# Four message-passing layers on a graph: the edge-MLP pass fetches three of every 32 chunks of source rows by products with node masks, and ScalarE's two relus change places

## The reference, cut to what matters

```
xi = x[dst]
xj = x[src]
h = jnp.concatenate([xi, xj - xi], axis=-1)
h = jax.nn.relu(h @ W1 + b1)
h = jax.nn.relu(h @ W2 + b2)
out = jax.ops.segment_max(h, dst, num_segments=x.shape[0])
```

## Time and profile before

| | |
|---|---|
| median of three runs | 10778.5 us |
| the profiled execution's own time | 10698.97 us |
| its span, first to last instruction | 10697.2 us |
| busy: PE / DVE / ACT / POOL | 4797.8 / 4232.9 / 1862.9 / 6552.4 us |
| granted TensorE clock, mean over the span | 0.653 |

### The profile page before, as it was taken

One profiled execution on the slowest core, in us unless ns is written; L12 is line 12 of the kernel. 1 busy time (PEld: TensorE's weight loads), 2 busy tenths in 40 slices (PEclk: granted clock), 3 DMA queues, 4 the chain that ended last, 5 costly groups with the idle time before them and its releaser, 6 DMA issues.

```text
span 10697.2 us, 122041 instructions
## 1 busy us (share of the span) xinstructions
PE 4797.8 (45%) x31058; PEld 3606.8 (34%) x31058; DVE 4232.9 (40%) x8620; ACT 1862.9 (17%) x5090; POOL 6552.4 (61%) x6391
## 2 busy tenths in 40 slices
PE   3788455555555457777777411211112311211111
PEld 3677444444444435555555211111111111111110
DVE  7899544445444554444444211212212111211212
ACT  0677223223322200000000100000000100000000
POOL 8333466666666545666665466666666566666666
PEclk9999655555555578898889655555555655555555
DMA  6000133333333312222222222222222222222222
GB/s 262 23 15 15 38 87 89 89 88 90 89 89 88 80 45 64 64 64 65 64 64 65 81 58 56 60 55 59 59 54 59 87 56 59 58 57 57 58 58 55
DMA packets 491880, 728.06 MB, mean 68 GB/s; under 512 B 143188, under 2 KB 206036, under 8 KB 488933
## 3 DMA queue, kind: packets, MB, share of 16 engines
q0 software_dynamic: 204288, 216.96, 11.8%
q1 hardware_dynamic: 159948, 245.16, 7.3%
q10 hardware_dynamic: 127584, 265.22, 6.5%
HBM read 421.77 MB, written 305.03 MB: 68 GB/s over the span
## 4 chain that ended last, share of the span: by engine, by line
another core or an unknown queue 36%; issue 21%; PE 21%; DVE 11%; POOL 4%; ACT 3%; DVEq 2%; DMA 2%; ACTq 0%; SPq 0%; POOLq 0%
PE ps L1672 8%; PE ps L1736 3%; DVE scn L1328 2%; PE ps L1704 2%; PE ps L1581 2%; PE ps L1548 1%; DVE shared L1308 1%; POOL big L723 1%; PE ps L1553 1%; DVE idx L1293 1%; POOL big L786 1%; DMA flags<-keep_and_type_rows 1%; DVE picked_nodes L1267 1%; POOL gat L776 1%
## 5 line engine op out<-in xcount | busy, mean ns | idle before, releaser
L776 POOL DMA_INDIRECT gat<-typed_table,idx x3128 | 2997.6, 958 | 1569.8 <-issue 918.2
L776 POOL DMA_INDIRECT gat<-node_table,idx x2835 | 2732.4, 964 | 1753.7 <-issue 857.7
L1736 PE MATMUL ps<-ident,scn 128*128 128x128 f32 x3136 | 938.3, 395 | 3543.4 <-DVE scn L1328 2335.8
L1328 DVE TENSOR_TENSOR_SCAN scn<-flags,scn,ps 128x256 f32<-128x256 bf16 x1176 | 874.0, 743 | 3510.1 <-remote 2966.3
L1736 PEld LDWEIGHTS ps<-ident,scn 128*128 128x128 f32 x3136 | 566.8, 226 | 3843.3 <-issue 3825.9
L863 ACT COPY dmp<-ps 128x256 f32<-128x256 f32 x1568 | 586.6, 374 | 6316.6 <-remote 3885.0
L1672 PE MATMUL ps<-big 128*128 128x320 bf16 x8820 | 1454.7, 319 | 147.1 <-issue 73.4
L1672 PEld LDWEIGHTS ps<-big 128*128 128x128 bf16 x8820 | 915.5, 104 | 550.3 <-issue 179.3
L1704 PE MATMUL ps<-ident,gat 128*128 128x128 f32 x3136 | 888.3, 380 | 443.2 <-DVE gat L1298 299.0
L1721 PE MATMUL ps<-shared,bd_w 128*128 128x256 f32 x784 | 447.6, 673 | 988.8 <-issue 596.2
L1704 PEld LDWEIGHTS ps<-ident,gat 128*128 128x128 f32 x3136 | 529.6, 193 | 558.9 <-issue 507.1
(11 more groups left out here) (287 smaller groups left out, 6087.5 us busy)
## 6 DMA issues: line engine op xcount, KB each, us to landing
scan_rows<-dmp ACTq DMA_DIRECT2D x784, 256.0 KB
flags<-keep_and_type_rows SPq DMA_DIRECT2D x980, 128.0 KB
spread_table<-tsl ACTq DMA_DIRECT2D x101, 576.0 KB, 15.9
shared<-spread_table SPq DMA_DIRECT2D x196, 288.0 KB
gat<-typed_table,idx POOLq DMA_INDIRECT x3128
gat<-node_table,idx POOLq DMA_INDIRECT x2835
typed_table<-shared SPq DMA_DIRECT2D x20, 1280.0 KB
group_rows<-node_group_rows SPq DMA_DIRECT2D x98, 128.0 KB
```

Of the source, the lines that this page charges most:

```text
L776: nc.gpsimd.indirect_dma_start(gat[:, k, g // ST, g % ST, :], None, table[:, :], bass.IndirectOffsetOnAxis(ap=idx[:, k, g:g + 1], axis=0)) ...
L1328: v.tensor_tensor_scan(scn[:, 1 - b, :], kept, values, scn[:, b, SH - 1:SH], ALU.mult, op).then_inc(s_scan, 1)
L1736: last = nc.tensor.transpose(bank(2 + b1)[:, g * P:g * P + P], by_edge(scn[:, b1, :], g), ident[:, :])
```

## The change

Three edits, all for pass 1. `BY_PRODUCT[1]` becomes `(1, 4, 6)`: in three of every eight steps the fourth chunk comes by products. The picks of the next step's chunk stand at the beginning of VectorE's step, behind the index copy, and not at its end. ScalarE's relu of the product stands ahead of its relu of the sums.

```diff
-BY_PRODUCT = {1: (), 2: (0, 1, 2, 4, 5, 6), 3: (), 4: ()}
+BY_PRODUCT = {1: (1, 4, 6), 2: (0, 1, 2, 4, 5, 6), 3: (), 4: ()}
...
-                    if q == MLP and live(1):
-
-                        act.wait_ge(s_hsum, s)
-                        nc.scalar.activation(hsm[:, 1 - b, :], hsm[:, 1 - b, :], ACT.Relu).then_inc(s_relu, 1)
                     if q == MLP and live(2):
 
                         act.wait_ge(s_mlp, s - 1)
...
                         nc.scalar.copy(inv_s[:, bass.ds((s - 2) * G, G)], bank(6)[:, SH:SH + G]).then_inc(s_wev, 1)
+                    if q == MLP and live(1):
+                        act.wait_ge(s_hsum, s)
+                        nc.scalar.activation(hsm[:, 1 - b, :], hsm[:, 1 - b, :], ACT.Relu).then_inc(s_relu, 1)
...
                     if q == MLP and live(0):
 
+                        s1, c1, n1, there = place(s, c, n, 1)
+                        if there:
+                            pick_nodes(q, s1, c1, n1)
                         dve.wait_ge(s_turn, nth(q) * NS + s + 1)
...
                         for ahead, work in ((1, pick_nodes), (3, mask_groups)):
                             s1, c1, n1, there = place(s, c, n, ahead)
-                            if there:
+                            if there and not (q == MLP and ahead == 1):
                                 work(q, s1, c1, n1)
```

## The result

The changed kernel takes 10732.16 us (median of seven runs, 10729.96 to 10743.35), the kernel before 10775.98 us in the runs beside it. The ratio is 0.9964, 95% interval 0.9953 to 0.9976: **faster by 0.36%, or 39 us** (the two medians lie 43.8 us apart), where 112 us were forecast. The profiled execution took 10738.40 us, six above the median.

What follows compares the result with a forecast made beforehand. POOL's gathers were taken as nearest to a bound in pass 1, filling 5.0 of 6.06 us a step. -184 + 92 - 45 + 10 + 15 = -112 us from 10778.5 gave 10665 us, range 10520 to 10860.

Steps and rivals of the forecast that it cites:

- What the waits give back: Pass 1, POOL: longer waits return half of what fewer gathers save, a share taken from passes 2 and 4; +92 us.
- DVE's new work: Pass 1, DVE: masks and picks, 1.84 us a product step, stay hidden by POOL's gathers; 0 us.
- PE's new work: Pass 1, PE: 30 products a chunk fit into an eight's time if the clock is up; 0 us.
- the beginning: Start of pass 1: splitting the table delays the first index copy, 15.7 us at most; +10 us.
- SP's queue: Pass 1, SP: group numbers loaded behind the flags may delay a mask once in every eight, at most 73 us; +15 us.
- the loop through PE: Rival, pass 1: 12 products waiting for a mask hold up the second weights' product; +61 us, 10840 us, chance 0.12.
- The gathers removed: Pass 1, POOL: 147 fewer gathers at 1.25 us each; -184 us if POOL's waits stay as they are.
- The reorder: Pass 1, ACT: product's relu first spares the maximum's scan a wait; a quarter of at most 180 us taken, -45 us.
- The clock: Pass 1, PE: products raise the granted clock from 0.56 to 0.75 or more.
- POOL isn't the bound: Rival, pass 1: the loop of DVE, ACT and PE sets the step, fewer gathers gain nothing; 10780 us, chance 0.12.

Runs made afterwards that it cites:

- h1: The kernel before, unchanged, run against itself for its profile on a third chip, one without unexplained PE stops: 9248.47 us, ratio 0.9997.
- e1: Against the kernel before, only ScalarE's relu of the product moved ahead of its relu of the sums, no products in pass 1: 10651.06 us, ratio 0.9964.

## Why the prediction was wrong

The sign and the range held; the size did not: -39 us for -112. Two steps failed, in opposite directions, by 92 us and by some 150, and cancelled in part. That the sign held is luck: without stops the same kernel is slower, 1.0055 and 1.0068.

**"What the waits give back", +92 us: 0.** With the gathers left out POOL's waits were 0.94 us a step after 0.95, and the time fell by the whole of their price (177 to 184 us). In the changed kernel the waits did rise, to 1.38 us, but for the products' loop and not for want of gathers. Lending the half from passes 2 and 4 was the mistake. Their steps differ in the rest of the work, and pass 2's step holds products.

**"DVE's new work" and "PE's new work", 0 each, with 25 us for the beginning and SP's queue: some 178 us.** This is the difference of the change (0.9964) and the gathers left out for nothing (0.9798), 1.66% of 10684 us, to some 20 us either way, as the two ratios come from two chips. I weighed busy time against the step, 40.4 us of PE in an eight of 46, and not the loop. The loop is mask, 12 products, second weights, relu, maximum, mask. That was the rival "the loop through PE", for which I had worked out 2.6 us at full clock against 2.65 of slack and let it pass as just covered. That slack was 6.06 - 3.41 us, and the 6.06 have the stops in them; the step without stops is 5.05 us, which leaves 1.64. It is not covered, even at the clock of 0.95 that the stretch has without stops, though the rival had asked for a clock under 0.75. What of the 178 us the runs place, with stops: 62 us go with the late load and the products' place; the gathers' longer mean, 979 ns against 956 with the reorder alone in 1600 to 3400 us, is 1418 x 0.023 = 33 us; the beginning of the pass is 16 us. The remaining 67 us are not placed. Without stops the loop costs the 175 us worked out above, and nothing of that size stays open.

**The gathers removed, -184 us**: right, with 146 gathers for 147 (1418 in the pass for 1564; the last eight had one of the three left out already).

**The reorder, -45 us**: -33 us with stops; +19 us without. The price came near for chips with stops, but the quarter was a choice, so that is luck. The reorder is not a saving of its own that can be added: it is worth 1.4% beside the change's products and nothing beside well placed ones.

**The beginning, +10 us**: the first index copy of a step comes at 1308.92 for 1286.89, in an execution that had been 5.8 us late before it, so +16.

**SP's queue, +15 us**: the mask waits 60.0 us in 1800, some 80 in the pass, above the upper end (73) of what I gave. But alone it buys nothing back with stops, and 0.2% without, since the products still stand ahead of the second weights.

**The clock**: as forecast, 0.82 for 0.75 or more. The rule on the clock that the prediction took from the Trainium skill, "TensorE: Matmul & The Clock Gate", Part 1, agrees with it in sign; a faster clock was not what was short. The other, in Part 3, that matmuls keep their order, was the one to weigh heavier: 326.3 us of 1400 without stops <-DVE big L1256 ahead of L1674 hold L1723 too.

**"POOL isn't the bound"**, which I drew from rows that showed nobody waiting for gathers, is refuted with stops by the gathers left out, and without stops the same kernel shows PE waiting 464.0 of 1400 us for them.

## What to carry to other kernels

Work that is added to an in-order engine must be weighed against the slack of the loop that it stands in, not against the engine's idle share: 12 products behind a mask undid a gain that 30 products behind the critical one left standing. If a trace holds long waits that nothing explains, a full ring is no proof that its producer isn't the bound; leave the producer's work out once and see what it gives. Remove two faults of a loop together before judging either: each alone gave 0.2% here without stops, both gave 1.7%.

## What the runs showed of the hardware

**One program has two levels, 15 to 17% apart**: 10684 to 10797 us on some chips, 9248 to 9253 us on three others. With stops, in the profile before, PE stands idle for over 0.5 us ahead of a matmul, with nothing in the profile to wait for, 428 times and 1976 us in all; without stops (h1), once. Among the 8236 pairs of successive products in pass 2 there are 49 gaps over 0.5 us with stops, 49.0 us in all, and one without, at the beginning of the pass. They keep to places in PE's program. Counted from the first matmul of an eight (212 records), 35 of the 49 stand at the 77th to the 83rd; and ahead of the 39th, a turn of gathered rows, PE stops in 37 of the 49 eights, most often for 1.6 us. The reorder alone, with stops (e1), has them at the same places (28 of its 38 at the 76th to the 83rd, 38 of 49 eights ahead of the 39th). What makes them wasn't tried and stays open.

**A gather slows under VectorE.** Of 1109 gathers before, without stops (1500 to 2900 us), 71 took over 1.0 us, up to 1.38, and all of them ran beside the scan of the maximum. With the reorder alone it was 128 of 1093, beside the same scan. With products behind it was 209 of 1076, up to 1.56 us, and all ran beside the scan of the maximum or a mask; the 651 gathers that met neither took 0.96 us at most. In the changed kernel's timeline on such a chip:

```profile
2402.42 0.74 DVE L1330 TENSOR_TENSOR_SCAN scn<-flags,scn,shared 128x256 f32<-128x256 bf16 x1
2402.61 1.31 POOL L776 DMA_INDIRECT gat<-node_table,idx  x1 [0.30 <-issue]
2404.22 0.94 POOL L776 DMA_INDIRECT gat<-node_table,idx  x1 [0.30 <-issue]
```

The gather that starts inside the scan takes 1.31 us, the next, beside an idle VectorE, 0.94. The Trainium skill may have the mechanism in "SBUF — State Buffer", "SBUF: two separate sides": VectorE and GpSimd share one port pair as an exclusive lock, which a VectorE instruction takes in a two-port mode, or, against a GpSimd instruction that reads SBUF, with two inputs in SBUF. The rows agree in part: this scan reads flags and relu's output from SBUF, and the mask group numbers and their constants, and the gather reads its indices there. But the products by type (L1314) read two tiles in SBUF too, and of the 234 gathers that ran beside them and not beside the scan none took over 0.95 us. So the mechanism isn't shown. It cost 0.04 us a gather with products, 55 us in the pass, three tenths of the 184 that they bring.
